# A graph layer's gathers: one column of ten blocks a layer loaded row by row from another queue

## What is computed

```python
q = (xn @ wq[l] + bq[l]).reshape(n, H, DH)      # H = 8 heads of DH = 32
k = (xn @ wk[l] + bk[l]).reshape(n, H, DH)
v = (xn @ wv[l] + bv[l]).reshape(n, H, DH)
scores = jnp.einsum('ehd,ehd->eh', q[dst], k[src]) * scale
m = jax.ops.segment_max(scores, dst, num_segments=n)
ex = jnp.exp(scores - m[dst])
z = jax.ops.segment_sum(ex, dst, num_segments=n)
attn = ex / z[dst]
agg = jax.ops.segment_sum(attn[:, :, None] * v[src], dst, num_segments=n)
```

## Time and profile before

| | |
|---|---|
| median of 3 runs | 3245.79 us (3243.38 to 3247.71) |
| the profiled execution | 3242.17 us |
| its span, first to last instruction | 3240.4 us |
| GpSimd busy | 1887.3 us, 58% |
| VectorE busy | 2453.7 us, 76% |
| TensorE busy | 2259.8 us, 70% |
| ScalarE busy | 1346.2 us, 42% |

### The profile page before, as it was taken

How to read it: one execution, slowest core, us unless ns; L and a number is a source line. 1 busy time by engine, 2 the same in 40 slices (tenths; PEclk the granted TensorE clock), 3 DMA queues, 4 the chain that set the end, 5 groups by cost and what they waited for, 6 DMA issues and landing times. The chain is left out here.

```text
span 3240.4 us, 28159 instructions
## 1 busy us (share of the span) xinstructions
PE 2259.8 (70%) x7343; PEld 1533.4 (47%) x7343; DVE 2453.7 (76%) x3912; ACT 1346.2 (42%) x3939; POOL 1887.3 (58%) x2002
## 2 busy tenths in 40 slices
PE   7746666666566656899966666666666666799998
PEld 4423333434333433576643343434343334577776
DVE  5778888888888888645358888888888888555334
ACT  4434444454544444212224444445444444222322
POOL 6167777777777777412057777777777777421000
PEclk9866777676767777899976767666677777799999
DMA  5377787777777777423257878777877777432111
GB/s 153 107 201 237 244 244 244 243 244 244 243 243 244 247 246 234 126 71 88 76 180 237 244 243 244 244 243 244 243 244 244 244 243 240 127 81 48 54 32 40
DMA packets 249862, 623.48 MB, mean 192 GB/s; under 512 B 50374, under 2 KB 105893, under 8 KB 249708
## 3 DMA queue, kind: packets, MB, share of 16 engines
q0 software_dynamic: 149904, 471.38, 49.2%
q1 hardware_dynamic: 99804, 150.30, 14.8%
HBM read 526.66 MB, written 94.78 MB: 192 GB/s over the span
## 5 line engine op out<-in xcount | busy, mean ns | idle before, releaser
L847 POOL DMA_INDIRECT ring<-kv_table,stage_ix x1760 | 1677.8, 953 | 588.2 <-issue 530.1
L1150 PE MATMUL bank<-ring,hot_w 128*128 128x272 f32 x1760 | 716.0, 546 | 509.9 <-DVE ring L2209 457.9
L1137 PE MATMUL bank<-qs,hot_q 128*128 x1760 | 691.6, 535 | 361.1 <-DVE ring L2180 302.0
L1150 PEld LDWEIGHTS bank<-ring,hot_w 128*128 128x128 f32 x1760 | 420.6, 260 | 787.9 <-DVE ring L2209 615.7
L2180 DVE TENSOR_TENSOR ring<-ring,bank 128x1024 f32<-128x1024 f32 x440 | 532.4, 1210 | 282.8 <-DMA ring<-kv_table,stage_ix 255.8
L1137 PEld LDWEIGHTS bank<-qs,hot_q 128*128 128x128 f32 x1760 | 444.4, 263 | 515.1 <-issue 425.7
L2185 DVE TENSOR_REDUCE s<-ring 128x32 f32<-128x1024 f32 x440 | 532.1, 1209 | 4.2
L1389 ACT ACTIVATE hot_q<-pos_b,row_of 128x128 f32<-128x128 bf16 x880 | 301.0, 392 | 21.1 <-DVEq L2168 12.0
L2197 DVE TENSOR_TENSOR bank<-ring,bank 128x512 f32<-128x512 f32 x420 | 286.3, 682 | 0.0
L2194 DVE TENSOR_TENSOR ring<-ring,bank 128x512 f32<-128x512 f32 x420 | 282.7, 673 | 0.0
L2209 DVE TENSOR_TENSOR ring<-ring,bank 128x512 f32<-128x512 f32 x420 | 280.5, 668 | 0.0
(11 more groups left out here) (363 smaller groups left out, 2370.1 us busy)
## 6 DMA issues: line engine op xcount, KB each, us to landing
agg_d<-stage_o SPq DMA_DIRECT2D x108, 544.0 KB, 4.4
ring<-kv_table,stage_ix POOLq DMA_INDIRECT x1760, 3.8
pos_b<-rel_d SPq DMA_DIRECT2D x54, 256.0 KB, 5.6
kv_table<-ring SPq DMA_DIRECT2D x50, 224.0 KB
h_dram<-ring SPq DMA_DIRECT2D x15, 560.0 KB
ring<-h_dram SPq DMA_DIRECT2D x15, 560.0 KB
ring<-in_x_dram SPq DMA_DIRECT2D x10, 560.0 KB
ring<-kv_table SPq DMA_DIRECT2D x10, 560.0 KB
```

The costliest lines, as they stand in the source:

```text
L847: gps.indirect_dma_start(out=chunk[:, par * G + i, j, :], out_offset=None, in_=table, in_offset=bass.IndirectOffsetOnAxis(ap=stage_ix[:, p ...
L1137: mm = ten.matmul(q_bank(third, i)[:, 0:QC], hot_q[:, i % 4, a * P:(a + 1) * P], qs[:, bass.ds(t * QC + a * QC, QC)], start=(a == 0), stop ...
L1150: mm = ten.matmul(b_acc[i % 2][:, lo - OWN:MC], hot_w[:, i % 4, :], chunk[:, s, j, lo:ROW], start=(j == 0), stop=(j == QD // 2 - 1), skip_ ...
```

## The change

Ten blocks of each layer, 20, 40, ..., 200, become "lone" blocks: GpSimd gathers three of their four columns. The fourth is loaded by SyncE, one row at a time: for each of the 128 partitions it loads the source's number from `src_ix` into a register and issues a DMA of that one row of 512 numbers into the partition's row of a buffer outside the ring. There are two buffers, used in turn: a new one of 128 x 512, and the unused part behind the query tiles. VectorE's operations on a lone block are done in two pieces, one for the ring and one for the buffer. `landed` counts the gathers of a slot, with the lone blocks' missing ones taken off.

SyncE issues 57 rows before the steps of a layer, and 19 at each of up to three places in a step, until 1280 are out. A buffer is filled for block i of the ten when the block two before it is weighed ("weighed"). Three waits come before a layer's first row: for the table's landing, and in layer 0 for `src_ix` and the end of the opening.

Two semaphores are merged into others to make place for "lone0" and "lone1": "quads_in" into "rows_in", "gate_in" into "w_in_dma" (whose total for the pass "last" becomes 36).

```diff
+LONE = tuple(range(20, 201, 20))
+LONE_ROWS = 19
+def landed(n):
+    layer, b = divmod(n, NB)
+    slot = b % SLOTS
+    lone = layer * sum(x % SLOTS == slot for x in LONE) + sum(x % SLOTS == slot for x in LONE if x <= b)
+    return 16 * (QD * (layer * uses(slot) + b // SLOTS + 1) - lone)
...
+        lone0 = sb("lone0", [P, ROW])
+        lone = (lone0[:, :], qs_f[:, QT * QC:QT * QC + ROW])
...
             def edges(layer):
+                filled = [0]
+                def fill(n):
+                    for at in range(filled[0], min(filled[0] + n, len(LONE) * P)):
+                        i, p = divmod(at, P)
+                        if p == 0 and (i >= 2 or layer):
+                            sp.wait_ge(S["weighed"], layer * NB + LONE[i - 2] + 1 - (0 if i >= 2 else NB))
+                        c = LONE[i] * QD + QD - 1
+                        row = nc.values_load(src_ix[p:p + 1, c:c + 1], engines=[mybir.EngineType.SP], min_val=0, max_val=N - 1,
+                                             skip_runtime_bounds_check_because="sources of edges are numbers of nodes")
+                        sp.dma_start(lone[i % 2][p:p + 1, :], kv_out[bass.ds(row, 1), :]).then_inc(S[f"lone{i % 2}"], 16)
+                    filled[0] += n
...
                     if nn == G:
                         sp.wait_ge(S["near"], k * G + (layer * NB + G))
                         positions(k + 2, par, blocks_of(k + 2))
+                    fill(LONE_ROWS)
                     if not first:
                         put(k - 1, 1)
+                        fill(LONE_ROWS)
                     if nn == LASTG:
-                        sp.wait_ge(gath[(NB - 1) % SLOTS], (layer + 1) * uses((NB - 1) % SLOTS) * QD * 16)
+                        sp.wait_ge(gath[(NB - 1) % SLOTS], landed(layer * NB + NB - 1))
                         next_weights()
                     if nn:
                         put(k, 0)
+                        fill(LONE_ROWS)
...
+                sp.wait_ge(S["kv_out"], (layer + 1) * NT * ROWS)
+                if not layer:
+                    sp.wait_ge(S["src_made"], 1)
+                    sp.wait_ge(S["pass_over"], 1)
+                fill(3 * LONE_ROWS)
                 in_groups(step)
...
-                        for j in range(QD):
+                        for j in range(QD - 1 if k * G + i in LONE else QD):
                             gps.indirect_dma_start(out=chunk[:, par * G + i, j, :], out_offset=None, in_=table,
...
-                    v.wait_ge(gath[s], turn * (QD * 16) + (layer * uses(s) + 1) * QD * 16)
+                    v.wait_ge(gath[s], landed(n))
                     v.wait_ge(S["self_copied"], n + 1)
+                    if n - b0 in LONE:
+                        i_, mine = lone_of(n)
+                        v.wait_ge(S[f"lone{i_ % 2}"], (layer * (len(LONE) // 2) + i_ // 2 + 1) * P * 16)
+                        q = q_bank(third, i)[:, 0:D]
+                        k_ = chunk[:, s, 0:QD - 1, 0:D]
+                        tt(k_, k_, q.rearrange("p (a w) -> p a w", a=1).to_broadcast([P, QD - 1, D]), ALU.mult)
+                        tt(mine[:, 0:D], mine[:, 0:D], q, ALU.mult).then_inc(S["q_used"], 1)
+                        return
...
+                        vec.tensor_reduce(s5[:, par, i, :, 0:QD - 1].rearrange("p h j -> p j h"),
+                                          chunk[:, par * G + i, 0:QD - 1, 0:D].rearrange("p j (h d) -> p j h d", h=H), AX.X, ALU.add)
+                        vec.tensor_reduce(s5[:, par, i, :, QD - 1], mine[:, 0:D].rearrange("p (h d) -> p h d", h=H), AX.X, ALU.add).then_inc(S["score"], 1)
...
+                        tt(two[:, 0:1], val[:, 2:3], w[:, 2:3].to_broadcast([P, 1, DH, H]), ALU.mult)
+                        tt(two[:, 1], mine[:, D:ROW].rearrange("p (d h) -> p d h", h=H), w[:, 3].to_broadcast([P, DH, H]), ALU.mult).then_inc(S["weighed"], 1)
```

More of the change, by code:

```diff
@@ L366, in program @@
         assert o <= QSPACE, o
+        lone = (lone0[:, :], qs_f[:, QT * QC:QT * QC + ROW])
+        assert QT * QC + ROW <= QSPACE
         z_pad = ring[0:29, at_late:at_late + 7 * QC]
@@ L377, in program @@
             "pool_const", "dst_in", "src_in", "ends_in", "pads", "prep", "prep_pe", "cuts_made", "ql_out", "quads_out",
[L378 removed]
+            "rows_in", "hots", "slot_ix", "src_made", "pens_made", "pens_out", "pad_out",
             "w_sq_in", "w_in_dma", "w_pe", "w_dve", "w_step", "kv_out", "h_out", "q_out", "q_in", "out_done", "pass_over", "edges_over",
@@ L381, in program @@
             "chain", "lanes", "ends_kept", "weights", "z_sum", "weighed", "w_ready", "wpos_near", "wpos", "agg", "evac", "agg_out0", "agg_out1", "agg_out2", "agg_out3", "ix_staged", "ix_group",
-            "l_pe", "l_dve", "l_act", "l_in", "l_home", "l_put", "first0", "first1", "first2", "first3", "first4",
-            "route", "gate_in", "ups_in0", "ups_in1", "downs_in", "route_pe", "route_act", "chosen")}
+            "lone0", "lone1", "l_pe", "l_dve", "l_act", "l_in", "l_home", "l_put", "first0", "first1", "first2", "first3", "first4",
+            "route", "ups_in0", "ups_in1", "downs_in", "route_pe", "route_act", "chosen")}
         gath = [sem(f"gath{s}") for s in range(SLOTS)]
@@ L388, in program @@
             if k in ONLY.get(n, PASSES)} for k in PASSES}
-        W_TOTAL = {"in": 8, "mid": 24, "last": 32}
+        W_TOTAL = {"in": 8, "mid": 24, "last": 36}
         PASS_NO = {"in": 0, "mid": 1, "last": 2, "moe": 3}
@@ L686, in next_weights @@
                 load_w("last", 1)
[L687 to L690, removed]
+                sp.dma_start(w_qkv[:, 0, 0:2 * NEXP].rearrange("p (a n) -> p a n", a=2), A["L0_ffn_Wr"].rearrange("(a p) n -> p a n", p=P)).then_inc(S["w_in_dma"], 16)
+                sp.dma_start(row_qkv[0:1, 0:NEXP], A["L0_ffn_br"].rearrange("(a n) -> a n", a=1)).then_inc(S["w_in_dma"], 16)
+                sp.dma_start(row_qkv[0:1, D:2 * D], A["L0_ffn_gamma"].rearrange("(a n) -> a n", a=1)).then_inc(S["w_in_dma"], 16)
+                sp.dma_start(row_qkv[0:1, 2 * D:3 * D], A["L0_ffn_beta"].rearrange("(a n) -> a n", a=1)).then_inc(S["w_in_dma"], 16)
             edges(1)
@@ L737, in quads_of_blocks @@
                     gps.indirect_dma_start(out=e_pack[:, a, :, :].rearrange("p e j -> p (e j)"), out_offset=None, in_=runs,
-                                           in_offset=bass.IndirectOffsetOnAxis(ap=e_quad_ix[:, a:a + 1], axis=0)).then_inc(S["quads_in"], 16)
+                                           in_offset=bass.IndirectOffsetOnAxis(ap=e_quad_ix[:, a:a + 1], axis=0)).then_inc(S["rows_in"], 16)
             def opening():
@@ L1246, in _ @@
             mm.then_inc(S["route_pe"], 1)
-            pe.wait_ge(S["gate_in"], 64)
+            pe.wait_ge(S["w_in_dma"], 16 * W_TOTAL["last"])
             pe.wait_ge(S["route"], R_MEAN)
@@ L1801, in opening @@
                             elif j == 3:
-                                v.wait_ge(S["quads_in"], 32)
+                                v.wait_ge(S["rows_in"], NT * 16 + 32)
                                 expand(6)
@@ L2171, in edges, with lone_of @@
                 g0, b0 = layer * NGRP, layer * NB
+                def lone_of(n):
+                    i = LONE.index(n - b0)
+                    return i, lone[i % 2]
                 def scores(par, i, turn, n, third):
                     s = par * G + i
-                    v.wait_ge(gath[s], turn * (QD * 16) + (layer * uses(s) + 1) * QD * 16)
+                    v.wait_ge(gath[s], landed(n))
                     v.wait_ge(S["self_copied"], n + 1)
+                    if n - b0 in LONE:
[6 more added lines that the diff above has]
+                        return
                     k_ = chunk[:, s, :, 0:D]
@@ L2184, in sum_scores @@
                     v.wait_ge(S["q_used"], n + 1)
+                    if n - b0 in LONE:
+                        _, mine = lone_of(n)
+                        vec.tensor_reduce(s5[:, par, i, :, 0:QD - 1].rearrange("p h j -> p j h"),
+                                          chunk[:, par * G + i, 0:QD - 1, 0:D].rearrange("p j (h d) -> p j h d", h=H), AX.X, ALU.add)
+                        vec.tensor_reduce(s5[:, par, i, :, QD - 1], mine[:, 0:D].rearrange("p (h d) -> p h d", h=H), AX.X, ALU.add).then_inc(S["score"], 1)
+                        return
                     vec.tensor_reduce(s5[:, par, i, :, 0:QD].rearrange("p h j -> p j h"),
```

## The result

The changed kernel takes **3963.02 us** (median of 6 runs; the kernel before beside it 3242.84 us): a ratio of 1.2226, 95% interval 1.2213 to 1.2239. Forecast were 3305 us, at most 3570. The direction came as written, and the path from SyncE to GpSimd is in the trace; the size did not, and two further waits came with it.

A forecast was written before the change was run, and what follows sets the result against it. GpSimd's gather issue was taken to bound the kernel. With 0.74 us a row on SyncE, each layer gains 29.5 us, +59 in all: 3242.2 + 59 + 3.6 = 3305 us, range 3216 to 3570 us.

The forecast's parts named there:

- The bound: Edge stages: GpSimd's gather issue, 1.254 us each without a break, sets the pace at 40.1 us a step.
- the whole possible gain: GpSimd: 20 gathers removed at 1.254 us each, 12.5 us a layer, 25.1 us in all.
- the place of the rows: SyncE: rows fill its sleep in order with stores, 57 a step, until the 1280 are out in step 21.
- the stores that are late next: SyncE's stores put(k, 0): ScalarE may not rewrite that half of stage_o until they land; 67.2 us late at put(21, 0).
- the costs taken as nothing: VectorE's splits (9 us, hidden), SyncE's new waits, the rows' traffic and merged semaphores: no cost to the time.
- The formula: Change per layer: 1197 c - 856.3 us, c SyncE's price of a row; -12.5 if the bracket is negative; +29.5 at 0.74.
- Both ends, 0.68 and 0.85: SyncE's price of a row in us: 0.68 without the MOVE and its gap, 0.85 if the first reader waits for the value.
- the reader's wait: Rival on SyncE: the reader waits for the loaded value, 0.85 us a row, +161 us a layer, 3568 us; chance 0.20.
- keep pace: Rival: SyncE at 0.68 us a row makes no store late; the 25.1 us arrive, 3221 us; chance 0.35.
- The third: Rival: SyncE's load slower among the gathers' traffic, 0.6 us instead of 0.31, 1.03 us a row, 3999 us; chance 0.03.
- What is lost is not won back: Behind step 21 of a layer GpSimd sets the pace again, so the +29.5 us a layer remain.
- the lateness: Delay of SyncE's store put(21, 0) in layer 1: 67.2 us at 0.74 us a row, of which 36.5 us are hidden.

The follow-up runs named there:

- one load a block: Changed kernel with one register load for each 128 rows instead of 128, so most rows copy the wrong source: 3214.31 us, ratio 0.9925.
- half of the loads: Changed kernel with one register load for every two rows, each second row repeating the first one's source: 3215.54 us, ratio 0.9922.
- loads first: Changed kernel with only the order altered, the 19 register loads of one fill before its 19 rows: 3391.45 us, ratio 1.0464.
- three loads in four: Changed kernel with three of four rows loaded, every fourth repeating the source of the row before it: 3582.64 us in one run.
- the probes: Kernel before with extra SyncE register loads, amid gathers and in a quiet stage: unused values 3241.86 us; two with used values 13 and 20 us over it.

## Why the prediction was wrong

**What held.** The bound (GpSimd's issue), the whole possible gain, the place of the rows, the stores that are late next, and the costs taken as nothing: one load a block gave all 25 us with everything else in place. The formula held too. The table takes c as (step - 1.2) / 57 from the stores of layer 1, and "measured" is the growth from first to last gather of layer 1 against the 1102.8 us before:

| kernel | step, us | row c, us | 1197c - 856.3, or -12.5 | measured |
|---|---|---|---|---|
| half of the loads | 41.14 | 0.701 | -12.5 | -14.7 |
| loads first | 45.41 | 0.776 | +72 | +72.6 |
| three loads in four | 50.01 | 0.856 | +169 | +165.4 |
| the change | 58.67 | 1.008 | +351 | +355.0 |

The formula follows four prices to within 5 us, and the break-even of 0.715 us lies where the runs put it, between 0.701 and 0.776. Price and growth are read from the same trace, so the table tests the count of rows and the slack, not the price.

**What failed** first of all is one term of the sum, the load: "the second TENSOR_LOAD of L701 takes 283 ns, with its gap 0.31 us". It measured 509 ns in the median and 534 in the mean, 0.56 with its gap; that is 0.25 of the 0.27 us by which the row was short (1.008 instead of 0.74). Both ends, 0.68 and 0.85, were built on the same 283 ns, so the range could not hold the time. The trace offered 479 ns in the same row, L701's first load, and 1935 ns for TensorE's eight; the MOVE and the reader's wait were given ends, but the load itself got no upper end except in a rival of 0.03. As the probes show, the first load was the one that is like the change's. With 0.479 in place of 0.283 the row would have been 0.94 us and the time, by the formula, some 3775.

Three smaller things were not as written. SyncE was to be on time at put(0, 0); at 1.008 us its 76 rows took 76 us, and that store went out 11.5 us later after the first gather than before the change. The arrival of the columns and of the positions was given no wait. And behind step 21 the stores did not go out 40 us apart: in layer 1 they came 16.0, 31.7 and 34.4 us apart, while SyncE caught up.

**The rivals.** SyncE does not keep pace: the MOVE is issued for every row (29 ns), and no overlap makes up for the load. The reader does not wait for the value: FUSED_REGOPS behind the load takes 37 ns, not 157. The third, the slow load, was what happened. Its 3999 us were nearest, but that is in part luck: its reason, the gathers' traffic, is excluded by the quiet stage. The Trainium skill's page "DMA: Bandwidth & Descriptors", section "Latency and other measured facts", has a floor of about 600 ns, amortized by unrolling. I set "the trace's 283 ns" against it. The runs are under that floor, 509 ns behind a row's DMA and 268 behind another load, but the change's own price was nearer to it than to 283. That loads can share a price agrees with the runs: loads in a row, and 792 ns for eight values by one load.

**"What is lost is not won back"** came out nearly as summed, but by two errors that cancel. Put(21, 0) of layer 1 was 403.5 us later than before, counted from the first gather, against 388 by the formula at c = 1.008; most of these 15 us are the 11.5 at put(0, 0). And 403.5 - 355.0 - 12.5 + 11.3 = 47 us of the lateness were hidden, not 36.5. That the formula is within 5 us for the change is to that extent luck.

## What to carry to other kernels

A sequencer's row of small instructions is priced from the sequence itself: a duration taken from another place counts only if the same instructions stand ahead of it, and here the last one was not enough. Where a queue must pass a thousand such rows a layer, each hundredth of a microsecond in one row is worth a dozen microseconds there. Put register loads side by side, or bring many values by one load, before the DMAs that use them. And a column that is filled ahead must have its last row out well ahead of its reader: 43 rows came late here, 70 did not.

## What was not expected of the hardware

A register load on SyncE takes, in the median, 268 to 274 ns behind another load, 282 when only a DMA of 128 short rows stands between it and the load before, 501 to 516 right behind a DMA of one row, and 443 when eight semaphore instructions stand between; amid gathers and without them alike. Behind a store it took 472, with a row's DMA before the store, and 468 and 448 as the first load of a layer. Why a single row between two loads does this was not tried further and stays open. So does why the second load of a fill took 928 ns on average in the change, where those of the other places took 488 to 519. Eight neighbouring words by one load take SyncE 756 to 805 ns in the probe; TensorE's eight took a typical 1935. Unused register loads left no record in the trace at all.
